# A transformer block on one core: where sixteen strings of slot scatters stand on the GpSimd queue

## What is computed

```python
def _dispatch_compute(xf, top_expert, w1, w2, capacity):
    ...
    indices = jnp.argsort(top_expert)
    ...
    xe = jnp.where(valid[..., None], xf[tok_idx], 0.0)
    h = jax.nn.gelu(jnp.einsum('ech,ehf->ecf', xe, w1), approximate=True)
    ye = jnp.einsum('ecf,efh->ech', h, w2)
    ...
    out = jnp.zeros((tokens + 1, hs), xf.dtype).at[tok_safe.reshape(-1)].add(ye.reshape(-1, hs))
...
scores = jax.nn.softmax(xf @ router_w, axis=-1)
expert_weights, top_experts = jax.lax.top_k(scores, TOP_K)
for k in range(TOP_K):
    y = _dispatch_compute(xf, top_experts[:, k].astype(jnp.int32), w1, w2, capacity)
    out = out + y * expert_weights[:, k][:, None]
...
x = x + 0.5 * _L0_ffn_ref(_layernorm(x, axis=-1), ...)
x = x + _L0_attn_ref(_layernorm(x, axis=-1), ...)
x = x + 0.5 * _L0_ffn_ref(_layernorm(x, axis=-1), ...)
```

## Time and profile before

| | before |
|---|---|
| median of three runs | 2439.61 us |
| the profiled execution's own time | 2450.27 us |
| its span (first to last instruction) | 2448.5 us |
| mean granted TensorE clock over the span | 0.962 |
| TensorE busy | 2204.8 us, 90% |
| GpSimd busy | 1142.9 us, 47% |
| VectorE, ScalarE busy | 1344.1 us, 1006.4 us |
| 16 DMA engines, mean | 86 GB/s |

### The profile page before, as it was taken

The page is one execution under the profiler, slowest core; times in us unless marked ns, Lnnn a source line. Parts: engine busy times, 40 slices in busy tenths (PEclk is TensorE's granted clock), DMA queues, the critical chain, the costliest instruction groups (busy, mean ns, idle before and its releaser), DMA issues.

```text
span 2448.5 us, 57464 instructions
## 1 busy us (share of the span) xinstructions
PE 2204.8 (90%) x22468; PEld 1919.9 (78%) x22468; DVE 1344.1 (55%) x3312; ACT 1006.4 (41%) x2149; POOL 1142.9 (47%) x911
## 2 busy tenths in 40 slices
PE   6749998999999995999899999729999999999997
PEld 6738887999999995777677777628888899999997
DVE  7745443555555552578677786635444455555552
ACT  4433333444443442446545565423333344344442
POOL 4754766444444433223343333254677544444443
PEclk9999999999999998999999999859999999999999
DMA  8522433434344434101211111223333443433432
GB/s 334 209 72 47 92 73 81 80 96 100 79 97 85 92 75 112 34 24 72 72 38 55 55 72 56 71 78 80 77 79 76 96 98 81 100 78 96 98 82 29
DMA packets 129221, 209.40 MB, mean 86 GB/s; under 512 B 24876, under 2 KB 105328, under 8 KB 122864
## 3 DMA queue, kind: packets, MB, share of 16 engines
q0 software_dynamic: 57344, 69.21, 17.2%
q1 hardware_dynamic: 71696, 137.62, 16.3%
HBM read 136.03 MB, written 72.88 MB: 85 GB/s over the span
## 4 chain that ended last, share of the span: by engine, by line
PE 48%; DVE 4%; issue 3%; another core or an unknown queue 3%; ACT 1%; POOL 1%; DMA 1%; POOLq 0%; DVEq 0%; ACTq 0%
PE bank L630 15%; PE bank L641 14%; PE bank L714 9%; PE bank L802 3%; PE bank L835 1%; PE bank L770 1%; PE bank L619 1%; PE bank L785 1%; PE bank L874 1%; PE bank L820 1%; PE bank L732 1%; POOL slot_table L381 0%; DVE aw L1754 0%; DVE xnl L1728 0%
## 5 line engine op out<-in xcount | busy, mean ns | idle before, releaser
L1096 ACT ACTIVATE h<-bank 128x512 f32<-128x512 f32 x512 | 306.3, 598 | 934.2 <-PE bank L630 775.2
L1663 DVE CAST hh<-h 128x512 fp32r<-128x512 f32 x512 | 223.2, 436 | 776.3 <-ACT h L1096 670.7
L641 PE MATMUL bank<-w2h,hh 128*128 128x256 f32 x2048 | 586.3, 286 | 7.7 <-issue 7.4
L641 PE MATMUL bank<-w2l,hh 128*128 128x256 f32 x2048 | 582.7, 285 | 8.5 <-issue 8.3
L641 PE MATMUL bank<-w2h,hl 128*128 128x256 f32 x2048 | 582.7, 285 | 7.1 <-issue 6.8
L630 PE MATMUL bank<-xh,w1h 128*128 128x512 f32 x1024 | 412.7, 403 | 15.4 <-issue 9.2
L641 PEld LDWEIGHTS bank<-w2h,hh 128*128 128x128 f32 x2048 | 394.1, 192 | 30.1 <-issue 10.8
L641 PEld LDWEIGHTS bank<-w2l,hh 128*128 128x128 f32 x2048 | 394.5, 193 | 28.9 <-issue 11.7
L630 PE MATMUL bank<-xl,w1h 128*128 128x512 f32 x1024 | 409.6, 400 | 0.7 <-issue 0.6
L418 POOL DMA_INDIRECT xe<-xn_rows,tab x256 | 269.5, 1053 | 294.2 <-issue 261.8
L630 PE MATMUL bank<-xh,w1l 128*128 128x512 f32 x1024 | 403.8, 394 | 0.7 <-issue 0.6
(11 more groups left out here) (209 smaller groups left out, 3321.1 us busy)
## 6 DMA issues: line engine op xcount, KB each, us to landing
stg<-in_L_ffn_w SPq DMA_DIRECT2D x64, 1024.0 KB
xb<-acc SPq DMA_DIRECT2D x9, 1024.0 KB, 8.4
xa<-in_L_attn_x SPq DMA_DIRECT2D x8, 1024.0 KB, 14.0
xn_rows<-xa SPq DMA_DIRECT2D x8, 1024.0 KB
xn_rows<-xn_r SPq DMA_DIRECT2D x8, 1024.0 KB, 4.7
xr<-acc SPq DMA_DIRECT2D x7, 1024.0 KB, 5.4
out_rows<-xr SPq DMA_DIRECT2D x7, 1024.0 KB
slot_table<-pay,idx POOLq DMA_INDIRECT x256
```

The costliest lines, as they stand in the source:

```text
L641: last = pe.matmul(o, a[:, fj, s], c[:, fj, :], start=(fj == 0 and n == 0 and t % 2 == 0), stop=(fj == FJ - 1 and n == 2), skip_group_chec ...
L1096: act.activation(h32[fj % 2][:], bank[fj % 2][:], ACT.Gelu_apprx_tanh).then_inc(f.gelu, 1)
L1663: dve.tensor_copy(hh[:, fj, :], h32[fj % 2][:]).then_inc(f.hh, 1)
```

## The change

The 64 second-choice scatters of a round no longer stand as eight strings of eight behind the adds of groups 0 to 7. Six of them go with each of the groups 0 to 10: one between the second and third gather, one behind the fourth gather, and one behind each of the four adds. Group 10 has the last four. The scatters themselves, their order and their number are the same; so are gathers, adds and every wait. Pair 2 is written out now, and the loop is over pairs 3 to 6. The same is done in both rounds.

```diff
+                def second_slot(g, i):
+
+                    m = g * 6 + i
+                    if m < B * NT:
+                        if m % NT == 0:
+                            held(pool, R[r].pay, m // NT + 1)
+                        scatter(r, m // NT, (NT + m % NT,))
+
+                def gather(j, waits, g=None):
 
                     for sem, value in waits:
                         held(pool, sem, value)
                     for t in range(GT):
+                        if g is not None and t == 2:
+                            second_slot(g, 0)
                         pool.indirect_dma_start(
                             out=xe[j % 2][:, t, :], out_offset=None, in_=xn_d,
                             in_offset=bass.IndirectOffsetOnAxis(ap=tabu[:, j, t, 0:1], axis=0),
                             bounds_check=ROWS - 1, oob_is_err=True).then_inc(xes[j % 2], 16)
-
-                def add(p, j, end):
+                    if g is not None:
+                        second_slot(g, 1)
+
+                def add(p, j, end, g=None):
...
+                        if g is not None:
+                            second_slot(g, 2 + t)
...
                 def pair(p, last, late):
                     for j in range(GE):
                         g3 = j + 3
+                        g = p * GE + j if late else None
                         if not (last and g3 >= GE):
-                            gather(g3 % GE, [(tabs[g3 % GE], p * 16 + 16 * (g3 // GE) + 16), (f.xT, p * GE + j + 2)])
-                        add(p, j, last and j == GE - 1)
-
-                        if late and late[j] is not None:
-                            scatter(r, late[j], SECOND)
...
-                with pool.Fori(2, NP - 1) as p:
-                    pair(p, False, None)
-                pair(NP - 1, True, None)
+                            gather(g3 % GE, [(tabs[g3 % GE], p * 16 + 16 * (g3 // GE) + 16), (f.xT, p * GE + j + 2)], g)
+                        add(p, j, last and j == GE - 1, g)
+
+                for p in range(3):
+                    pair(p, False, True)
+                with pool.Fori(3, NP - 1) as p:
+                    pair(p, False, False)
+                pair(NP - 1, True, False)
```

More of the change, by code:

```diff
@@ L393, in half_bias @@
                 pool.tensor_tensor(x[:, two, :], x[:, two, :], hbias[:].unsqueeze(1).to_broadcast([P, 2, C]), ALU.add).then_inc(R[1].half, 1)
-            FIRST, SECOND = range(NT), range(NT, RT)
+            FIRST = range(NT)
             power(R[0], ln0[0], 0)
@@ L411, in ffn @@
                 tabu = tab[:].bitcast(u32)
-                def gather(j, waits):
+                def second_slot(g, i):
[5 more added lines that the diff above has]
+                def gather(j, waits, g=None):
                     for sem, value in waits:
```

## The result

| | before | after |
|---|---|---|
| median | 2440.58 us (4 runs) | 2400.48 us (4 runs, 2391.97 to 2404.43) |
| ratio | | **0.9844**, 95% interval 0.9805 to 0.9882 |
| profiled execution, its span | 2450.27, 2448.5 us | 2399.01, 2397.2 us |

The change won 40 us where 53.5 were forecast; 2400.5 us lies in the range, and even in the forecast case's own range of 2371 to 2407. The word **starvation** stands for the loss that goes with the strings; what does it inside the chip stays open.

A forecast was written before the change was run, and what follows sets the result against it. TensorE, busy 90% of the span, was taken as the bound, starved by GpSimd's unbroken chains in groups with strings. 68.5 at stake - 12 residue - 3 lateness = 53.5 us won: 2439.6 - 53.5 = 2386 us, range 2368 to 2448.

The forecast's parts named there:

- the forecast case: Spreading the scatters wins back most of the string groups' loss: 2386 us, own range 2371 to 2407, chance 0.62.
- What was at stake: The eight group periods with strings in each round lose 36.01 + 32.47 = 68.5 us, 2.8% of the run.
- The residue of starvation: Loss still left in the eleven groups with scatters after the change: between 0 and 36 us, taken as 12.
- GpSimd's cycle: GpSimd's time for a group with six spread scatters: 24.73 us, 1.29 more than TensorE's 23.44.
- The step that failed: SP's weight loads, queued behind its waits for the adds, reach `stg` a whole group before use, so count as free.
- The 3 us for the lag: GpSimd falls behind TensorE and gathers come late by 1.6 us at group 13; counted as 3 us for both rounds.
- the slack of the gathers: Group 4's gathers land by 233.6, TensorE wants them at 243.61: 10.0 us to spare.
- Every group clumps: Rival: the new 21.3 us GpSimd chain still starves TensorE in eleven groups a round; 25.7 us more, 2465 us; chance 0.17.
- A price for each scatter: Rival: each scatter costs 0.54 us wherever it stands, so no gain, 2440 to 2443 us; chance 0.09.
- Code loading: Rival: TensorE's gaps are waits for code on first passes of pair 0 and its loop; time stays 2440 us; chance 0.06.
- GpSimd becomes the bound: Rival: a 26 us GpSimd cycle makes `xe` late from group 8, 13 us lost a round; 2397 us; chance 0.06.

The follow-up runs named there:

- strings6: Changed kernel with each group's six scatters as one string behind the fourth add; 2336.77 us against 2339.01 for the kernel before, ratio 0.9997.
- tail4: Changed kernel with two of six scatters among the adds and four behind the last; 2338.36 us against 2339.01 for the kernel before, ratio 0.9996.
- no_second: Changed kernel without the 128 second-choice scatters and SyncE's wait for them; 2337.89 us against 2339.01 for the kernel before, ratio 0.9993.
- mixed: Changed kernel with six scatters behind the adds in round 0, two among and four behind in round 1; 2338.81 us against 2340.15 before.
- mixed_b: The kernel of mixed again, on a chip with starvation; 2410.28 us against 2455.51 for the kernel before, ratio 0.9814.
- after_c: The changed kernel, unchanged, on a chip without starvation; 2359.14 us against 2340.15 for the kernel before, ratio 1.0084.
- sp_early: Changed kernel with SyncE's weight loads in pairs 0 to 2 issued ahead of the wait for the adds; 2355.67 us against 2339.01 before, ratio 1.0073.
- after_again: The changed kernel, unchanged, beside the kernel before on another chip with starvation; 2399.72 against 2437.12 us, ratio 0.9851.

## Why the prediction was right, and where not

**What was at stake** was right: 68.5 us lost in the groups with strings, and 48.6 of them came back in the trace (68.5 - 19.9). On chips without starvation these groups lose nothing in the traces of strings6, tail4, no_second and mixed, the kernels that do not lag.

**The residue of starvation,** forecast as 12 us between bounds of 0 and 36, was 0. The lower bound was the true one. The reason given with it, that no run of scatters and gathers reaches 11 us, was only argued then; in the changed kernel the longest run is 8.4 us. The two rounds of mixed_b bear it out in part: they show that the placement decides, and not the number of scatters.

**GpSimd's cycle** was forecast as 24.73 us; it was 25.4. The first one was exact: 205.63 to 230.31, 24.7 us. Two of the ten have 6.4 and 6.5 us from the last add's end to the next gather in place of 5.06, since `tab` came later, and single operations ran up to 0.5 us longer.

**The step that failed** is "SP's weight loads, queued behind its waits for the adds, go into `stg` a whole group before they are used". The 3 us for the lag should have been 20, of which the same stretches now show 9.7 and 10.3 us. I had checked the slack of the gathers (10.0 us) and not that of the weights. It could be read from before. These lines are from the undisturbed group of the earlier trace rows, whose first add starts at 524.15:

```profile
534.37 0.43 SPq L276 DMA_DIRECT2D stg<-in_L_ffn_w  x1
...
547.56 0.41 ACT L1100 ACTIVATE w1h<-stg 128x256 fp32r<-128x256 f32 x1
```

The load is issued 13.2 us before ScalarE first uses it, and not a whole group (23.44 us). In the changed kernel it took 5.8 us from the issue to ScalarE's use (348.90 to 354.75). That leaves some 7.4 us, less than the 10.0 of the gathers. GpSimd's adds now take 11.4 us and not 7.5, and its lag grows by 2 us a group, so ScalarE waits from the third group on. What hid the load before was that GpSimd kept pace. That the lag is the cause, and not a price of the scatters, is shown by tail4 and by mixed beside after_c on one chip, with as many scatters in as many groups, a cycle that keeps pace and no loss at all; and by sp_early, where the wait moved from the weights to the gathers and the loss stayed.

**Luck.** Two errors nearly cancel: 12 us too many for the residue, 17 too few for the lag. The forecast set aside 12 + 3 = 15 us for both, and 0 + 19.9 us were lost. The number is near for a reason that the forecast did not have.

**TensorE was not the only one to stand still.** The prediction read TensorE's gaps alone. In the group of the earlier trace rows, in the trace of before, these are two activations of ScalarE in a row, and the end of TensorE's last hidden product ahead of its gaps:

```profile
304.75 1.09 ACT L1090 ACTIVATE xh<-bank 128x512 fp32r<-128x512 f32 x2 [1.31 <-remote]
312.60 0.60 ACT L1096 ACTIVATE h<-bank 128x512 f32<-128x512 f32 x1 [6.76 <-remote]
...
308.02 0.39 PE L630 MATMUL bank<-xh,w1l 128*128 128x512 f32 x1
```

ScalarE does nothing from 305.84 to 312.60, although one hidden product was done at 305.59 and the next at 308.41, and VectorE had been done with the buffer since 304.53; "remote" is the profile's word for a release by another core or by something that it does not know. ScalarE's rest starts 2.8 us before TensorE's first gap, and the fourth gap ends at 313.25, when ScalarE's activation has just made its bank free (313.20): the program has a wait for it there. So one part of the "nameless" 17.8 us, at line 630, is TensorE waiting for ScalarE; the gaps at line 641 lie inside products that wait for nothing, as the prediction had it. Over the eight periods such "remote" waits of ScalarE before line 1096 sum up to 63.5 us (15, longest 6.8); in the groups without strings there is none, nor in mixed on a chip without starvation. In mixed_b they are 63.7 us in round 0 and still 27.7 us in round 1, where TensorE loses 3.3: the lighter placement does not rid ScalarE of them, but few reach TensorE.

**The rivals.** *Every group clumps*: of nameless gaps one of 0.3 us is left in the first round's eleven groups, and none in the second's. *A price for each scatter*: mixed_b has the same scatters in both rounds and 23.7 against 3.3 us; the rival falls. *Code loading*: TensorE's program is the same in both rounds of mixed_b, and this rival has no reason for their difference. The Trainium skill, Runtime: NRT & Kernel Launch, section "Instruction fetch mechanics", has a sequencer fetch code by its own queue; no run here shows a wait that needs it. *GpSimd becomes the bound* is what happened in part: by way of the weights, and so from the third group on, not the eighth. Its number, 2397 us with no residue, was nearer to the 2400.5 than the forecast's 2386.

**The size** came out at 40 us for 53.5. In the trace the gain is 51.3 us, 2448.5 - 2397.2. But the profiled execution of before was 10 us slower than its median, and that of the changed kernel was not. The prediction took the trace's gain for that of the runs; this held only to 11 us. Of the 13 us between forecast and result, some 5 are the sum's (48.6 for 53.5) and the rest is this.

**What could not be foreseen** is that the gain depends on the chip. From the one trace it was a property of the kernel. Its range was right for the chip that it was made for and for that of after_again; on the chip of after_c the direction was wrong. On the other two chips without starvation the changed kernel itself was not timed.

## What to carry to other kernels

When work is moved onto an engine's chain, list every queue that waits for that chain's results, and read the slack of what is queued behind each of these waits, not only of the data on the direct way: here a load of weights had less slack than the gathers. A new item belongs where the engine rests: four scatters behind the last add fill a wait of 5 us, and with two among the adds the cycle keeps pace; with two among the gathers and three among the adds it is longer than TensorE's. Where a stall has no name in the profile, time both kernels on more than one chip before calling it a gain, and look at the waits of the other engines in the same stretch. Of the placements tried, two scatters among the adds and four behind them costs nothing on the two chips without starvation where it was timed alone, and 3.3 us in its round on a chip with it; in both rounds it was not timed on such a chip.

## What the runs showed of the hardware

The same program, before, had medians of 2440.58, 2437.12 and 2455.51 us in three sittings, and 2339.01, 2338.21 and 2340.15 us in three others, on other chips. The chip of the first measurement is not on record; the other five are five different ones. The packets of the software queue do not take longer on the first: in the changed kernel they took 17.6% of the 16 engines' span on the first chip and 18.0% on that of after_c, which is 422 and 424 us. The difference is in TensorE's nameless gaps and what follows them, and also in the attention layer. From the last transposes of round 0 to the first of round 1, before on the first chip, then the changed kernel (the same code there) on a chip without gaps:

```profile
912.50:1645.70 733.20, 609.82 (x12589) 483.66 (x12588) 480.63 (x1306) 342.26 (x658) 249.24 (x208) 0.91 0.19 61
...
885.24:1576.96 691.72, 589.82 (x12589) 471.36 (x12588) 479.22 (x1306) 342.67 (x658) 249.63 (x208) 0.93 0.20 65
```

41.5 us are lost there. With the 68.5 us this is 110 us, nearly as much as the traces of before and of tail4 differ (2448.5 - 2337.1 = 111.4). GpSimd issues strings of six in that layer, but that they are the cause of the 41.5 us is not shown: no kernel tried another placement there. 20 of them are TensorE's busy time, at a lower mean clock (0.91 for 0.93).

What it is in a string of indirect transfers that holds up TensorE and ScalarE, and why only on some chips, stays open. The Trainium skill, SBUF — State Buffer, section "SBUF: two separate sides", excludes that a DMA slows a compute engine at the memory. No run here tests that for the data; the runs show that the engines' loss goes with how GpSimd issues the transfers, on those chips.
